# Two layers of a graph kernel on one core: a third row group formed as seven block products, with GpSimd adding the blocks

## The reference

```python
h = relu(layernorm(x))                      # x: 5120 x 64
u = par_u[0]*par_u[1] * (diag_u[:,None] * h[:2048] @ W_u) + h[:2048]
i = par_i[0]*par_i[1] * (diag_i[:,None] * h[2048:] @ W_i) + h[2048:]
e = concatenate([u, i])                     # 5120 x 64
g = adj @ (adj.T @ e)                       # adj: 5120 x 5120, f32
out = x + layernorm(g) * gamma + beta + h
```

## Time and profile before

| | |
|---|---|
| median of three runs | 371.75 us |
| the profiled execution | 371.32 us |
| its span, first to last instruction | 369.5 us |
| TensorE busy | 360.3 us, 98% |
| VectorE busy | 263.0 us, 71% |
| GpSimd busy | 159.6 us, 43% |
| ScalarE busy | 74.3 us, 20% |
| read from memory | 131.55 MB |

### The profile page before, as it was taken

The page is one execution under the profiler, slowest core; times in us unless marked ns, Lnnn a source line. Parts: engine busy times, 40 slices in busy tenths (PEclk is TensorE's granted clock), DMA queues, the critical chain, the costliest instruction groups (busy, mean ns, idle before and its releaser), DMA issues.

```text
span 369.5 us, 10865 instructions
## 1 busy us (share of the span) xinstructions
PE 360.3 (98%) x4776; PEld 151.7 (41%) x4776; DVE 263.0 (71%) x282; ACT 74.3 (20%) x213; POOL 159.6 (43%) x94
## 2 busy tenths in 40 slices
PE   7998999999999999999999999999999999999994
PEld 4664454543323443443334334334433343344432
DVE  5999994999061969395677839694956768385266
ACT  5863022010050004001300500040023005002422
POOL 2023060020019902970793199049607931990036
PEclk9999999999999999999999999999999999999998
DMA  8999999999999978989898989889898989853933
GB/s 311 422 419 415 418 426 419 419 419 402 403 380 411 363 291 331 427 343 411 323 429 331 419 326 425 338 318 421 349 409 326 427 339 413 325 247 132 426 130 142
DMA packets 19897, 133.22 MB, mean 361 GB/s; under 512 B 2209, under 2 KB 2977, under 8 KB 4001
## 3 DMA queue, kind: packets, MB, share of 16 engines
q1 hardware_dynamic: 19440, 132.22, 88.1%
q10 hardware_dynamic: 432, 0.66, 0.5%
HBM read 131.55 MB, written 1.31 MB: 360 GB/s over the span
## 4 chain that ended last, share of the span: by engine, by line
PE 87%; DMA 7%; POOL 2%; SPq 2%; DVE 1%; issue 0%; ACT 0%; DVEq 0%; POOLq 0%
PE h_acc L887 36%; PE t_acc L918 24%; DMA natural<-adj_rows 7%; PE x_acc L955 7%; PE h_acc L975 7%; PE t_acc L856 5%; PE t_acc L955 5%; PE h_acc L870 2%; POOL xs L424 1%; SPq L289 1%; POOL sums L420 1%; PE t_acc L993 1%; DVE xs L795 0%; SPq L286 0%; DVE sums L784 0%
## 5 line engine op out<-in xcount | busy, mean ns | idle before, releaser
L599 DVE STREAM_TRANSPOSE strips<-natural 128x2048 f32<-128x2048 f32 x76 | 169.0, 2279 | 48.2 <-PE h_acc L887 48.0
L887 PE MATMUL h_acc<-strips,tokens 32*64 32x512 f32 x2432 | 133.5, 589 | 0.1
L918 PE MATMUL t_acc<-natural,e 128*32 128x512 f32 x832 | 92.3, 592 | 0.1
L887 PEld LDWEIGHTS h_acc<-strips,tokens 32*64 32x64 f32 x2432 | 53.3, 132 | 79.4 <-issue 74.3
L399 POOL TENSOR_TENSOR sums<-natural 128x1024 f32<-128x1024 f32 x14 | 33.3, 2381 | 113.4 <-DMA natural<-adj_rows 113.4
L918 PEld LDWEIGHTS t_acc<-natural,e 128*32 128x32 f32 x832 | 27.4, 110 | 59.4 <-issue 58.2
L955 PE MATMUL x_acc<-sums,forms 128*32 128x256 f32 x280 | 41.1, 380 | 0.0
L856 PE MATMUL t_acc<-natural,e 128*64 128x256 f32 x320 | 36.5, 382 | 1.4 <-DMA natural<-adj_rows 1.1
L489 ACT COPY smalls<-x_acc 32x256 f32<-32x256 f32 x7 | 2.6, 365 | 170.1 <-PE t_acc L955 170.1
L479 ACT COPY tokens<-tokens 32x384 f32<-32x384 f32 (+2 forms) x60 | 24.2, 403 | 51.6 <-DVE tokens L623 30.9
L407 POOL TENSOR_TENSOR sums<-natural,sums 128x1024 f32<-128x1024 f32 x14 | 33.3, 2379 | 1.1
(11 more groups left out here) (97 smaller groups left out, 299.8 us busy)
## 6 DMA issues: line engine op xcount, KB each, us to landing
natural<-adj_rows SPq DMA_DIRECT2D x100, 1024.0 KB, 7.9
cols<-adj_cols SPq DMA_DIRECT2D x20, 1024.0 KB, 11.6
natural<-adj_last SPq DMA_DIRECT2D x4, 1024.0 KB, 10.8
out<-xs SPq DMA_DIRECT2D x4, 256.0 KB, 2.0
xs<-x ACTq DMA_DIRECT2D x2, 256.0 KB, 5.3
xs<-x SPq DMA_DIRECT2D x2, 256.0 KB, 7.7
out<-xs SPq DMA_DIRECT2D x2, 128.0 KB, 2.0
smalls<-small SPq DMA_DIRECT2D x1, 150.0 KB, 3.6
```

The costliest lines, as they stand in the source:

```text
L599: nc.vector.transpose(strips[:, a, :, m].rearrange("p c t i -> p t c i"), natural[:, a, m].rearrange("p t (c j) -> p t c j", j=Q)).then_in ...
L887: last = nc.tensor.matmul(h_acc[D * s:D * (s + 1), q], t[part, a, b, u, :], rows, start=(isinstance(g, int) and g == 0 and b == 0 and u == 0),
L918: last = nc.tensor.matmul(t_acc[lane, pair_bank(half)].rearrange("p (a w) -> p a w", a=2), e[:, GT * m + 2 * k + s, Q * v:Q * (v + 1)], na ...
```

## The change

Group 1 joins groups 4 and 3's scheme, and group 2 takes the place of group 3: `SUMMED` is now (1, 4, 2), so 0 and 3 are plain. GpSimd adds twelve times per pair instead of eight. There is no further room for sums: groups 1 and 2 use the same four buffers in turn, so the sums of group 2 are not begun before TensorE has multiplied those of group 1 of the same pair, and those of group 1 not before group 2 of the pair before. The sums of group 1 are needed in `first_early`, which is a third of a round earlier than the sums of groups 4 and 2. VectorE turns in the order (0,1), (0,2), (0,0), (1,1), (0,3), (1,0), (1,2), finishes `t`, then turns (1,3); SyncE loads in the order (0,1), (0,0), (1,1), (0,4), (1,0), (1,4), (0,2), (1,2), (0,3), two `cols`, (1,3). `u` and `v`, two small intermediates of `t`, move from `x_acc` to `t_acc`, and `v` is formed before the first transposition of `t`, so that `x_acc` is free for group 1 of the next pair; TensorE waits for that (`s_v`).

```diff
-TURNS = (0, 1, 3, 2)
-BEHIND = 2
-SUMMED = (4, 3)
+TURNS = ((0, 1), (0, 2), (0, 0), (1, 1), (0, 3), (1, 0), (1, 2), (1, 3))
+BEHIND = 1
+SUMMED = (1, 4, 2)
...
-        u, sixth_rest, _, v = (x_acc[Q * lane:Q * (lane + 1), WIDE:2 * WIDE] for lane in range(QUADRANTS))
+        sixth_rest = x_acc[Q:2 * Q, WIDE:2 * WIDE]
+        u, v = (t_acc[0:Q, 1, WIDE * n:WIDE * (n + 1)] for n in range(2))
...
             for g in range(PAIRED + 2, PANELS, 2):
-                for a in range(2):
-                    for m in range(EARLY):
-                        refill(g + a, m)
-                for m in (4, 3, 2):
-                    for a in range(2):
-                        refill(g + a, m)
+                for a, m in ((0, 1), (0, 0), (1, 1), (0, 4), (1, 0), (1, 4), (0, 2), (1, 2), (0, 3)):
+                    refill(g + a, m)
                 for a in range(2):
                     refill_cols(g - 2 + a)
+                refill(g + 1, 3)
...
-                    pool.wait_ge(s_first, firsts_pair(half - 1, m))
+                    if m == 2:
+                        pool.wait_ge(s_first, firsts_pair(half, 1))
+                    else:
+                        pool.wait_ge(s_first, firsts_pair(half - 1, 2 if m == 1 else TURNED))
...
+                dve.wait_ge(s_v, 2 * (half - FIRST_HALF) - 1)
+                nc.vector.tensor_tensor(v, first_v, uv, ALU.add).then_inc(s_v, 1)
                 dve.wait_ge(s_t_left, left + 3)
                 turn_t(2 * half, 0, slice(0, WIDE))
-                dve.wait_ge(s_v, 2 * (half - FIRST_HALF) - 1)
-                nc.vector.tensor_tensor(v, first_v, uv, ALU.add).then_inc(s_v, 1)
...
-                turn_first(half)
-                for m in TURNS[:-BEHIND]:
-                    turn_strips(2 * half + 1, 1, half, m)
+                for a, m in TURNS[:-BEHIND]:
+                    turn_strips(2 * half + a, a, half, m)
                 t_ready(half)
-                for m in TURNS[-BEHIND:]:
-                    turn_strips(2 * half + 1, 1, half, m)
+                for a, m in TURNS[-BEHIND:]:
+                    turn_strips(2 * half + a, a, half, m)
...
             def first_rest(half):
                 first_summed(half, 4)
-                first_plain(half, 2)
-                first_summed(half, 3)
+                first_summed(half, 2)
+                first_plain(half, 3)
 
             def first_early(half):
-                for m in range(EARLY):
-                    first_plain(half, m)
+                first_plain(half, 0)
+                if not isinstance(half, int):
+                    pe.wait_ge(s_v, 2 * (half - FIRST_HALF - 1))
+                first_summed(half, 1)
...
+            pe.wait_ge(s_forms, FORMS * len(SUMMED))
             first_early(FIRST_HALF + 1)
-            pe.wait_ge(s_forms, 4 * len(SUMMED))
```

More of the change, by code:

```diff
@@ L36 @@
 EARLY = 2
-TURNS = (0, 1, 3, 2)
-BEHIND = 2
-SUMMED = (4, 3)
+TURNS = ((0, 1), (0, 2), (0, 0), (1, 1), (0, 3), (1, 0), (1, 2), (1, 3))
+BEHIND = 1
+SUMMED = (1, 4, 2)
 FORMS = 4
-SUMS = 4 * len(SUMMED)
+SUMS = FORMS * len(SUMMED)
 LEFT = 5
@@ L48 @@
 WARM = 4
-SCRATCH = 2048
+SCRATCH = 1024
 LN_EPS = 1e-5
@@ L192, in sums_done, with turns_of, turned_all @@
         def sums_done(half, m, n=4):
-            return SUMS * (half - FIRST_HALF - 1) + 4 * SUMMED.index(m) + n
+            return SUMS * (half - FIRST_HALF - 1) + FORMS * SUMMED.index(m) + n
         def turned_count(g, m):
-            return TURNED * g + (TURNS.index(m) if g >= PAIRED else m) + 1
+            if g < PAIRED:
+                return TURNED * g + m + 1
+            return TURNED * (g - g % 2) + turns_of(g - g % 2).index((g % 2, m)) + 1
+        def turns_of(g):
+            return [(a, m) for a, m in TURNS if g + a < LAST]
+        def turned_all(g, a):
+            if isinstance(g, int) and g < PAIRED:
+                return TURNED * (g + 1)
+            turns = turns_of(g) if isinstance(g, int) and g == LAST - 1 else TURNS
+            return TURNED * (g - a) + 1 + max(n for n, turn in enumerate(turns) if turn[0] == a)
         def block_of(a, m, s):
@@ L382, in _ @@
             pool.wait_ge(s_e_centred, GROUPS)
-            parts = e[:, GT * 3:GT * 5].rearrange("p (m k s) (v d) -> p m k s v d", m=2, s=2, v=2)
+            parts = e.rearrange("p (m k s) (v d) -> p m k s v d", m=GROUPS, s=2, v=2)
             for m in SUMMED:
-                low, high = (parts[:, m - 3, :, s] for s in range(2))
+                low, high = (parts[:, m, :, s] for s in range(2))
                 nc.gpsimd.tensor_tensor(form_of(m, 0), low[:, :, 1], low[:, :, 0], ALU.subtract).then_inc(s_forms, 1)
@@ L678, in turn_pair @@
             def turn_pair(half, t_ready):
-                turn_first(half)
-                for m in TURNS[:-BEHIND]:
-                    turn_strips(2 * half + 1, 1, half, m)
+                for a, m in TURNS[:-BEHIND]:
+                    turn_strips(2 * half + a, a, half, m)
                 t_ready(half)
-                for m in TURNS[-BEHIND:]:
-                    turn_strips(2 * half + 1, 1, half, m)
-            def turn_first(half):
-                for m in TURNS:
-                    turn_strips(2 * half, 0, half, m)
+                for a, m in TURNS[-BEHIND:]:
+                    turn_strips(2 * half + a, a, half, m)
             def keep_t_plain(half):
@@ L756, in _ @@
                 turn_pair(half, keep_t_pair)
-            turn_first(LAST_HALF)
+            for a, m in turns_of(LAST - 1):
+                turn_strips(LAST - 1, a, LAST_HALF, m)
             keep_t_pair(LAST_HALF)
@@ L877, in second_strips @@
             def second_strips(g, a, blocks=range(BLOCKS)):
-                pe.wait_ge(s_strips, TURNED * (g + 1))
+                pe.wait_ge(s_strips, turned_all(g, a))
                 pe.wait_ge(s_t, g + 1)
```

## The result

The changed kernel takes 384.63 us (median of four runs, 384.32 to 386.21) against 371.98 us for the kernel before, timed beside it; the ratio is 1.0351, 95% interval 1.0319 to 1.0382. It is 12.65 us slower. The profiled execution is the slowest of the four, 386.21 us, and 14.9 us longer than that of before, so its terms add up to some 2 us more than the medians differ.

A forecast was written before the change was run, and what follows sets the result against it. TensorE's work was taken to bound the kernel before the change, a closed loop through the load of (1,1) after it. 3.8 + 4.8 + 2.6 + 0.4 = 11.6 us onto 371.32 gave 382.9, forecast as 383, range 375 to 390.

The forecast's parts named there:

- a loop from strips to strips: In each round, strips, turn and load of (1,1), GpSimd's additions and the summed group follow in a chain: 34.6 us.
- Start, +3.8: Before the loop, TensorE waits for block (1,0) and group 1's sums; strips begin at 116.1 instead of 112.3 us.
- Each round, 29.43 + L: Round length in the loop: fixed steps plus a load's landing, 34.6 us, 0.8 more than before; +4.8 us over six rounds.
- L: Time from issue to landing of the load of (1,1): taken as 5.2 us, with 4.7 and 7.0 kept as alternatives.
- the wait for the fourth addition: Sign in the profile: TensorE waits for GpSimd's fourth addition just ahead of the strips in every round, about 1 us.
- Last round, +2.6 and +0.4: In the last round, group 2's sums come 2.6 us late, and v ahead of t's transposition adds 0.4 us.
- Clock: Rival: TensorE's clock falls in the new waits, 1.2 us lost per fall; 385 us with two falls, 394 with nine; 13%.
- Sums of groups 4 and 2: Inside the loop, these sums end at T + 6.5 and T + 16.1, before T + 13.9 and T + 16.95; T is the strips' start.
- the price that I bounded at 0 to 6 us: GpSimd's group 1 additions clashing with VectorE's work on t: 0 to 0.32 us each; taken as nothing.
- A form: One of four more 128 x 128 forms on GpSimd before its first block: estimated 0.3 us each, costing nothing.
- Saving, 0.44 us a group: A summed group takes TensorE 3.03 instead of 3.47 us; in seven pairs 3.1 us in all.
- The load of (1,0): In the loop, it lands about when plain group 0 wants it; a wait there is part of the wait behind it.

The follow-up runs named there:

- e3: Changed kernel, but TensorE starts a summed group after three of four sums, waiting for the fourth only where it is first read: 377.34 us.
- e5: Changed kernel, but VectorE turns (0,3) ahead of (1,1) instead of behind it: 395.73 us.
- e2: Changed kernel, but the last round takes groups 4, 3, 2 instead of 4, 2, 3: 381.69 us.
- e8: e4 with (1,0) turned fifth and loaded ahead of (0,4), and v formed at its old place in the last round: 370.84 us, ratio 0.9979 to the kernel before.
- e9: Changed kernel with only (1,0) moved earlier: turned fifth and loaded ahead of (0,4): 387.11 us.
- e4: Changed kernel with e2, e3, and pair 3's group 1 plain with its first loads as before: 374.08 us, ratio 1.0058 to the kernel before.
- e6: Changed kernel with only groups 4 and 2 summed, group 1 plain throughout, new orders kept: 380.46 us.

## Why the prediction was right

I forecast 383.0 us, 375 to 390; it is 384.63. The mechanism, a loop from strips to strips through the load of (1,1) and its sums, is shown by e3 and e5; that the number came so near is in part luck, as the steps show:

- *Start, +3.8.* Right: strips at 116.13 for 116.1 forecast, by way of the two waits named.
- *Each round, 29.43 + L.* Right in its mechanism (e5 lengthens the loop, e3 shortens it). The four middle rounds are 34.40 to 34.47, which is L = 4.8 with 0.2 us of small steps; I took 5.2. But the first round is 37.1: there L was 6.3 and the strips took 15.2 instead of 14.0 us. In all six rounds 209.4 us, 6.4 more than the 203.0 of before, for 4.8 forecast: five rounds came out shorter than I took them and one much longer. Also, I expected the wait for the fourth addition in every round; in two of the six the wait named is that for (1,0).
- *Last round, +2.6 and +0.4.* Right: 2.33 us for the sums, 0.57 for `t` where 0.13 was there before. e2 takes the first away.
- *Clock.* Held as a rival at 13%. It came true in part: one fall in the profiled execution, which lasted 3.4 us and cost 1.7, where I took 2.4 us and 1.2.
- *The rest.* Sums of groups 4 and 2 were in time inside the loop. GpSimd's additions beside the work on `t` took 2.35 to 2.39 us, so the price that I bounded at 0 to 6 us is nothing. A form took 0.46 us, not the 0.3 that I estimated, which cost nothing either: they were done at 86 us, 17 us before GpSimd's first block.
- *Saving, 0.44 us a group.* It was there but never seen in the changed kernel; e8 shows 0.40 a round.

The profiled execution's sum is 3.8 + 6.4 + 2.3 + 1.7 + 0.4 = 14.6 us of the 14.9 by which it is longer than that of before.

Two things the forecast had too small. The load of (1,0) appeared only as a part of the wait behind it, and so it is (e9), but it is a second limit just under the first: that is why e4 gained 4.3 us less than I expected. And e6 shows that the new orders alone cost 9 us, without any sum of group 1; while its profiled execution, 7.2 us longer than that of before, names waits of some 6. In my sum all of the loss, but for 0.4 us, followed from the sums.

Open is why the first strips took 15.2 us, with the clock at 1.00. They did in e2 too and about so in e5 (14.9), not in e3 and e9. Some 0.8 us of it is one pause of TensorE's weight loads (PEld), 1.06 us long where 0.25 is usual; the profile names nothing that ended it:

```profile
119.12 0.23 PEld L897 LDWEIGHTS h_acc<-strips,tokens 32*64 32x64 f32 x15 [1.06 <-issue]
```

In these three executions a packet of the instruction queue (q8) starts 0.3 to 0.5 us after the strips begin (here at 116.5 us); in e3 and e9 it comes 2.3 and 6.2 us ahead of them. That points to instructions arriving late, but no run tests it. Why the load took 6.3 us in the first round is open too.

## What to carry to other kernels

When a step is put between the landing of a load and its use, follow the buffer round: what frees it, who issues the load, how long to the landing. If that ring comes back to the work it feeds, its length is a lower limit for the round, however idle each engine is; here 29.4 us and a landing, against 33.4 us of work. An engine with room on average (28.8 of 33.4 us) is no argument: look at the first and last rounds, where the cover is thinner, and at which wait is next once the first is gone. A wait on the last of several inputs can be moved to where that input is first read (e3: three lines, 7 us).

## What the runs showed of the hardware

- A wait of 2.3 us on TensorE cost 1.6 to 1.7 us beyond itself, since the clock stood at 0.50 (1.2 GHz) for some 3.4 us behind it. So it was behind all five single waits of 2.27 to 2.50 us in the loop and the last round of the changed kernel, e5 and e9. The length alone doesn't decide: at the start, between 105 and 114 us, waits of 2.42 us (e5), 2.96 (the changed kernel) and 3.58 (e9) left the clock at 1.00. Why isn't known.
- Two waits of 1 us with 3.6 us of work between them left the clock up, where one of 2.27 us did not.
- A 1 MB load issued 2.6 us behind another landed after 4.8 to 5.0 us in five of the six rounds of the changed kernel and of e9, and after 6.3 us in the first.
- GpSimd's 84 additions of 128 x 1024 kept 2.35 to 2.40 us in the changed kernel, beside VectorE's turns and beside its work on `t`.
